# Last batch of a linear-attention layer: attention split by group of heads into the x buffers, output products in quarters, norms of unit 7 first

## The chip, the cores and the metric

One core of one Trainium2 chip runs the whole program. The metric is the device time of one execution in microseconds (us), lower is better. Engines: PE is TensorE (matmuls), DVE is VectorE, ACT is ScalarE, POOL is GpSimd, SP is SyncE (here it only issues DMAs).

## The reference, cut to what matters

Eight batches of 1024 tokens with 512 features, 16 heads of 32, 128 random features per head:

```python
q = feature_map(split(x @ Wq.T + bq), orf)      # exp(proj - norm) + EPS, norm from the row's squares
k = feature_map(split(x @ Wk.T + bk), orf)
v = split(x @ Wv.T + bv)
kv = jnp.einsum('nlm,nld->nmd', k, v)
ksum = jnp.sum(k, axis=1)
buf = jnp.concatenate([kv, ksum[..., None]], axis=-1)
out = jnp.einsum('nlm,nmd->nld', q, buf)
out = out[..., :-1] / out[..., -1:]
...
x = _layernorm(x + (out @ Wo.T + bo))
x = _layernorm(x + x @ (w_ternary * scale).T)
```

## The kernel before

**Units and groups.** The 16 heads are four groups of 4. Each group has two units of work: unit 2g makes the keys' features, unit 2g+1 the queries' features, so a batch has units 0 to 7. After unit 7 come the output stages, which take the 8 tiles of 128 tokens in turn.

**Order.** All engines walk one list, `SCHEDULE`, which `unit_stages` and `output_stages` write out; each engine does its own part of every stage, in that order, and waits on semaphores. The list decides what stands in front of what on each engine.

**Stages.** `P` projects a half unit into a bank of PSUM, in two parts of 6 matmuls. `S` (ACT) copies it as `unit_hi` and makes `squares`; `L` (DVE) makes `unit_lo`; `Q` (DVE) sums the squares; `N` (DVE) makes `norm_rows` from both sums. `LIFT` (SP's queue) moves hi and lo into `stacks`; `NL` (POOL's queue, 8 small DMAs) moves the norms there. A unit's feature stages `F` on PE wait for both. ACT takes the exponential of each `F` into `features`. For a key unit DVE adds the 8 tiles of features up (7 additions, L707 once and L710 six times, each waits for the one before). `G` are PE's products of features and values; the last of them (L910, "ones") also needs the sum of all 7 additions. ACT and PE then turn the result (`KVT`). `GG` is a half of a group's attention on PE, after which DVE turns and inverts the denominators (L783, L786, L789); `R` (L799, L801) writes a group's attention for four tiles (or, with a fourth number, two tiles) into `values_then_attention`.

**Output stages.** For each tile, `A` splits the attention into hi (ACT, L543) and lo (DVE, L715), and POOL adds the bias to the rows of x (L521); `O` is 12 matmuls with Wo; `LN` (DVE, L813 and L691 to L697) adds the rows and takes the statistics, POOL finishes the scale (L486, L488), ACT applies it (`Y`, L548); `YT` turns the tile (PE), ACT copies hi, DVE makes lo (L818); `FF` is 8 matmuls with the ternary weights, and DVE adds and takes statistics again (L823 and on); `ST` (ACT) scales and stores.

The hi and lo of `A` live in two slots each of `stacks`, so a tile's split waits for the output product two tiles back:

```python
if t < 2:
    act.wait_ge(t_f.sem, t_f.nth(b, 8 * NU))
else:
    act.wait_ge(t_o.sem, t_o.nth(b, t - 1))
```

In all but the last batch, unit 5 also splits the next batch's x (`XT`, on POOL for tiles 4 to 7, L515); the last batch has no such stages, and no projections of a next batch either.

Of the kernel before, what the change touches and what calls it, by code (L numbers as in the profile page):

```python
# [62 lines left out]
def unit_stages(b, u):  # L63
# [40 lines left out]
    if u < NU - 1:  # L104
# [3 lines left out]
        if u < NU - 3:  # L108
# [7 lines left out]
        return seq + [("R", b, g, 1)]  # L116
    v0 = [("V", b + 1, 0)] if two else []
# [4 lines left out]

def output_stages(b):

    more = b + 1 < B

    def v(t):
        return [("V", b + 1, t)] if more else []
# [3 lines left out]
    for t in range(3, TT):  # L132
# [4 lines left out]
        if t == 4 and more:  # L137
            seq += [("Q", b + 1, 1, 1), ("N", b + 1, 1)]
    seq += [("Y", b, TT - 1)] + v(TT - 1) + [("FF", b, TT - 2), ("ST", b, TT - 3), ("YT", b, TT - 1)]
    if more:  # L140
        return seq + [("P", b + 1, 2, 0, 0), ("P", b + 1, 2, 0, 1), ("LIFT", b + 1, 1), ("FF", b, TT - 1), ("NL", b + 1, 1)]
    return seq + [("FF", b, TT - 1), ("ST", b, TT - 2), ("ST", b, TT - 1)]
# [22 lines left out]
RING = {"V": "pj", "P": "pj", "O": "pj", "FF": "pj", "F": "ft", "YT": "ft"}  # L165
RING_SIZE = {"pj": 2, "ft": 3}


def bank_uses(seq):
# [3 lines left out]
    last = {ring: [(-1, None)] * size for ring, size in RING_SIZE.items()}  # L173
    held, out = {}, []
    for n, stage in enumerate(seq):
        ring = RING.get(stage[0])
        if stage[0] in ("S", "L"):
            out.append((held[("P", *stage[1:], 0)], None))
        elif stage[0] == "LN":
            out.append((held[("O", *stage[1:])], None))  # L180
        elif stage[0] == "P" and stage[4]:
            out.append((held[(*stage[:4], 0)], None))
        elif ring is None:
            out.append((None, None))
        else:
            mine = last[ring]
            bank = mine.index(min(mine, key=lambda use: use[0]))
            held[stage] = bank
            out.append((bank, mine[bank][1]))
            reader = {"P": ("L", *stage[1:4]), "O": ("LN", *stage[1:])}.get(stage[0], stage)  # L190
            mine[bank] = (at[reader], stage)
# [3 lines left out]
def attention_kernel(nc, x, xt, wq, wk, wv, wo, wff, bias, bo, orf, out):  # L195
# [5 lines left out]
    with ctx:  # L201
# [47 lines left out]
        BANKS = {"pj": PS[0:2], "ft": PS[2:5]}  # L249
# [35 lines left out]
        g_xb = Signal("x_plus_bias_ready", TT)  # L285
        g_ln = [Signal("ln1_scale_ready", 2 * TT), Signal("ln2_scale_ready", 2 * TT)]
# [46 lines left out]

        def x_rows(t):
# [3 lines left out]
        def old_bank(stage):  # L338
# [6 lines left out]
            if kind == "O":  # L345
                return v_ln[0], v_ln[0].nth(b, 5 * k + 1)
# [8 lines left out]
        def steps():  # L355

            for stage, (bank, old) in zip(SCHEDULE, BANKING):
                ps = None if bank is None else BANKS[RING.get(stage[0], "pj")][bank]
# [97 lines left out]
        def _(pool):  # L456
# [51 lines left out]
            for kind, b, at, _, _ in steps():  # L508
# [3 lines left out]
                elif kind == "XT" and b and t >= 4:  # L512
# [3 lines left out]
                                            ALU.subtract).then_inc(g_xlo.sem, 1)  # L516
                elif kind == "A":
# [10 lines left out]
        def _(act):  # L528
# [16 lines left out]
            def apply_norm(k, b, t):  # L545
                act.wait_ge(g_ln[k].sem, g_ln[k].nth(b, 2 * t + 2))
                row = XR[:, t % 4, :]
# [3 lines left out]
            for kind, b, at, ps, _ in steps():  # L551
# [61 lines left out]
                elif kind == "A":  # L613
                    split_hi(b, u)
                elif kind == "Y":
# [379 lines left out]
```

## Time and profile before

| | |
|---|---|
| median of 3 runs | 1331.96 us (1330.17 to 1334.98) |
| profiled execution | 1332.59 us, of which span 1330.8 us |
| PE busy | 96% of the span |
| DVE, ACT, POOL busy | 75%, 52%, 36% |
| last batch's units 5 to 7 and output stages | from about 1239 us to the end |

Times in the trace count from the start of the span. A busy PE is not PE at its peak, since matmuls overlap. `[idle before <-releaser]` at the end of a row is the engine's idle time ahead of it, and what ended it. The column PEclk is the granted TensorE clock, where 1.00 is 2.4 GHz and 0.50 is 1.2 GHz.

### The profile page before, as it was taken

The numbers are of one execution on the slowest core, as the hardware profiler recorded it, in microseconds if no ns is written. First come the engines' busy times: TensorE is split into PE (matmuls) and PEld (weight loads), VectorE is DVE, ScalarE is ACT, GpSimd is POOL, SyncE is SP. The second block draws the span as 40 slices with busy tenths as digits, with TensorE's granted clock in tenths as the row PEclk, the third lists the DMA queues.
The fourth block names the chain that finished last, engine by engine and source line by source line (L and its number), as shares of the span: only waits on it lengthen the run. The fifth ranks groups of instructions, "written<-read, shape, count | busy, mean of one in ns | idle before, by whom it ended". The sixth has DMA issues, their size and how long they took to land.

```text
span 1330.8 us, 25104 instructions
## 1 busy us (share of the span) xinstructions
PE 1280.9 (96%) x8522; PEld 962.9 (72%) x8522; DVE 996.5 (75%) x2077; ACT 695.6 (52%) x1337; POOL 476.1 (36%) x877
## 2 busy tenths in 40 slices
PE   6999999999999999999999999999999999999786
PEld 5766688677877768776787768876688667886564
DVE  5688875787767886688757887578876788758876
ACT  5466535565355643556436663366544664355543
POOL 1233432354333343234423343234442344332433
PEclk9999999999999999999999999999999999999999
DMA  5467503673146631468215662257602674046511
GB/s 205 128 144 195 137 33 96 170 190 93 52 110 167 174 87 54 107 159 209 60 56 127 170 170 67 60 138 203 156 25 75 168 192 122 33 116 138 139 47 48
DMA packets 94014, 160.35 MB, mean 120 GB/s; under 512 B 31168, under 2 KB 47680, under 8 KB 93376
## 3 DMA queue, kind: packets, MB, share of 16 engines
q1 hardware_dynamic: 67712, 139.51, 40.8%
q10 hardware_dynamic: 9792, 17.12, 3.4%
q0 software_dynamic: 16384, 2.13, 1.1%
q8 instruction: 68, 1.11, 0.4%
q14 instruction: 58, 0.48, 0.1%
HBM read 39.13 MB, written 16.78 MB: 42 GB/s over the span
## 4 chain that ended last, share of the span: by engine, by line
PE 81%; DVE 8%; ACT 4%; issue 3%; DMA 2%; SPq 2%; POOL 1%; ACTq 0%; DVEq 0%; POOLq 0%
PE ps L835 28%; PE ps L872 23%; PE ps L933 7%; PE ps L904 4%; PE ps L858 4%; PE ps L860 4%; PE ps L859 4%; PE ps L891 3%; PE ps L949 2%; ACT features L599 1%; DVE cols L786 1%; DVE squares_turned L753 1%; DVE cols L757 1%; DVE stacks L715 1%; ACT x_hi L568 1%
## 5 line engine op out<-in xcount | busy, mean ns | idle before, releaser
L599 ACT ACTIVATE features<-ps 128x512 f32<-128x512 f32 x512 | 278.6, 600 | 270.6 <-PE ps L835 198.6
L505 POOL DMA_DIRECT2D stacks<-norm_rows x512 | 252.0, 500 | 420.5 <-DVE norm_rows L768 169.4
L486 POOL TENSOR_TENSOR stats<-stats,cols 128x1 f32<-128x1 f32 x128 | 79.0, 617 | 377.9 <-DVE stats L697 377.9
L835 PE MATMUL ps<-Wo_hi,stacks 128*128 128x512 f32 x512 | 173.3, 402 | 5.8 <-DVE stacks L715 3.7
L710 DVE TENSOR_TENSOR den<-den,features 128x512 f32<-128x512 f32 x192 | 134.6, 701 | 15.4 <-ACT features L599 2.1
L573 ACT ACTIVATE values_then_attention<-ps 128x512 f32<-128x512 f32 x64 | 38.2, 598 | 200.2 <-PE ps L860 197.4
L835 PE MATMUL ps<-W_ternary,stacks 128*128 128x512 f32 x512 | 127.9, 392 | 6.9 <-DVE stacks L818 6.9
L835 PE MATMUL ps<-orf_key_a,stacks 128*128 128x256 f32 x512 | 132.3, 289 | 1.6 <-DMA stacks<-norm_rows 1.6
L933 PE MATMUL ps<-features,kv_ksum 128*32 128x512 f32 x1024 | 123.1, 598 | 8.4 <-ACT features L599 5.6
L835 PE MATMUL ps<-orf_key_b,stacks 68*128 68x256 f32 x512 | 129.0, 283 | 0.0
L548 ACT ACTIVATE rows<-rows,stats 128x512 f32<-128x512 f32 x128 | 100.9, 813 | 42.4 <-POOL stats L488 42.2
L835 PEld LDWEIGHTS ps<-Wo_hi,stacks 128*128 128x128 f32 x512 | 96.1, 188 | 35.5 <-DVE unit_lo L745 8.5
L835 PEld LDWEIGHTS ps<-orf_key_a,stacks 128*128 128x128 f32 x512 | 97.6, 191 | 27.5 <-issue 23.4
L835 PEld LDWEIGHTS ps<-W_ternary,stacks 128*128 128x128 f32 x512 | 96.0, 189 | 28.3 <-issue 4.7
L745 DVE SCALAR_TENSOR_TENSOR unit_lo<-ps,cols,unit_hi 128x512 fp32r<-128x512 f32 x128 | 94.2, 736 | 28.3 <-ACT squares L583 27.6
L858 PE MATMUL ps<-Wv_hi,x_hi 128*128 128x512 f32 x256 | 103.8, 406 | 11.7 <-DVE x_lo L738 10.9
L872 PE MATMUL ps<-x_hi,Wk_hi 128*128 128x512 f32 x256 | 106.9, 418 | 0.0
L872 PE MATMUL ps<-x_hi,Wq_hi 128*128 128x512 f32 x256 | 101.5, 396 | 2.1 <-DVE unit_lo L745 2.1
L872 PE MATMUL ps<-x_lo,Wq_hi 128*128 128x512 f32 x256 | 101.9, 398 | 0.0
L872 PE MATMUL ps<-x_hi,Wq_lo 128*128 128x512 f32 x256 | 101.4, 396 | 0.0
L872 PE MATMUL ps<-x_hi,Wk_lo 128*128 128x512 f32 x256 | 101.2, 395 | 0.0
L859 PE MATMUL ps<-Wv_lo,x_hi 128*128 128x512 f32 x256 | 101.0, 395 | 0.0
(113 smaller groups left out, 2615.6 us busy)
## 6 DMA issues: line engine op xcount, KB each, us to landing
stacks<-unit_hi SPq DMA_DIRECT2D x384, 128.0 KB, 2.5
stacks<-unit_lo SPq DMA_DIRECT2D x256, 128.0 KB, 3.3
stacks<-unit_hi SPq DMA_DIRECT2D x64, 256.0 KB, 3.8
out<-rows ACTq DMA_DIRECT2D x64, 256.0 KB, 2.0
rows<-in_x_t SPq DMA_DIRECT2D x56, 256.0 KB, 3.6
stacks<-norm_rows POOLq DMA_DIRECT2D x512, 4.0 KB, 2.6
rows<-in_x SPq DMA_DIRECT2D x32, 256.0 KB, 3.8
features<-in_x SPq DMA_DIRECT2D x32, 256.0 KB, 3.8
```

What stands on the lines that cost most here:

```text
L486: nc.gpsimd.tensor_tensor(ln(k, t, 10), ln(k, t, 8), EXPO, ALU.pow).then_inc(g_ln[k].sem, 1)
L505: pool.dma_start(slot[row:row + 1, c:c + L].rearrange("o (t c) -> o t c", c=DH), NN[DH * h:DH * (h + 1), u % 2, part, :].bitcast(F32)).the ...
L548: nc.scalar.activation(row, row, ACT.Identity, scale=ln(k, t, 10), bias=ln(k, t, 11))\
L599: nc.scalar.activation(FE[:, n % 8, :, 0:M], ps[:, :].rearrange("p (a m) -> p a m", a=HG), ACT.Exp, scale=C_EXP).then_inc(a_exp.sem, 1)
L710: ins = nc.vector.tensor_tensor(total, total, FE[:, r, :, 0:M], ALU.add)
L745: nc.vector.scalar_tensor_tensor(out=EL[:, u % 2, half], in0=ps[:, :], scalar=BC[:, u:u + 1], in1=EH[:, u % 2, half].bitcast(F32), op0=ALU ...
L835: last = mm(out, a, b, start=(n == 0), stop=(n == len(terms) - 1))
L858: mm(ps[:, :], XH[:, k, c], WH["v"][:, k, :], start=(k == 0), stop=False)
L859: mm(ps[:, :], XH[:, k, c], WL["v"][:, k, :], start=False, stop=False)
L860: last = mm(ps[:, :], XL[:, k, c], WH["v"][:, k, :], start=False, stop=(k == KT - 1))
L872: last = mm(ps[:, :], *terms[n], start=(n == 0), stop=(n == len(terms) - 1))
L933: last = mm(bank[DH * h:DH * (h + 1), :], KVS[:, g % 2, c + DH * h:c + DH * (h + 1)], FE[:, HG * half + h, :, 0:M], start=True, stop=True, ...
```

## The change

Only the last batch changes. In its unit 5, unit 7's projections, squares and norms come ahead of group 2's attention (`GG`, `R`). The attention of each group is split as soon as it exists (new stage `AG`), for four tiles at once, into the buffers `x_hi` and `x_lo`, which no projection needs any more: hi on ACT; lo on POOL for groups 0 to 2, and on DVE, two tiles at a time, for group 3. The output product of a tile is cut into four quarters (new stage `OK`, 3 matmuls for one group) that can run apart; the first ones run inside unit 7. The normed rows stay in `values_then_attention`, the turned ones go into `x_hi` and `x_lo`, and all five banks serve all of these stages. The order of the output stages is another one (`last_output_stages`).

```diff
-        if u < NU - 3:
+        if b + 1 == B and u == NU - 3:
+            seq += p[1] + s0 + l0 + kv + f(2, 3) + p[2] + f(4, 5) + s1 + q0 + [("KVT", b, g)] + f(6, 7) + l1 + [("GG", b, g, 0)] + q1 + norm + lift
+            seq += [("GG", b, g, 1), ("R", b, g, 0)] + [("LR", b, t) for t in range(4)]
+            seq += [("AG", b, k, h) for k in range(2) for h in range(2)]
+        elif u < NU - 3:
...
+    if b + 1 == B:
+        seq = [("AG", b, 2, 0), ("AG", b, 2, 1)] + f(0, 1, 2) + [("OK", b, 0, 0)] + kv + f(3) + [("OK", b, 1, 0), ("KVT", b, g)]
+        seq += f(4, 5) + [("A", b, t) for t in range(4)] + [("GG", b, g, 0), ("R", b, g, 0, 0), ("AG", b, g, 0, 0)] + f(6, 7)
+        seq += [("OK", b, t, k) for k in (1, 2) for t in (0, 1)] + [("R", b, g, 0, 1), ("AG", b, g, 0, 1)]
+        seq += [("OK", b, 0, 3), ("LN", b, 0), ("OK", b, 1, 3), ("LN", b, 1), ("GG", b, g, 1)]
+        seq += [("OK", b, 2, k) for k in range(KT)] + [("LN", b, 2), ("Y", b, 0), ("A", b, 4)]
+        return seq + [("LR", b, t) for t in range(4, TT)]
...
+def last_output_stages(b):
+
+    def o(t, *chunks):
+        return [("OK", b, t, k) for k in chunks or range(KT)]
+
+    g = NG - 1
+    seq = o(3) + [("R", b, g, 1, 0), ("AG", b, g, 1, 0), ("YT", b, 0), ("LN", b, 3), ("Y", b, 1), ("A", b, 5)]
+    seq += o(4, 0, 1, 2) + [("YT", b, 1), ("FF", b, 0), ("R", b, g, 1, 1), ("AG", b, g, 1, 1), ("Y", b, 2), ("A", b, 6), ("A", b, 7)]
+    for t in range(4, TT):
+        seq += o(t, 3) + [("LN", b, t)] + (o(t + 1, 0, 1, 2) if t + 1 < TT else []) + [("YT", b, t - 2), ("ST", b, t - 4), ("Y", b, t - 1), ("FF", b, t - 3)]
+    seq += [("YT", b, TT - 2), ("ST", b, TT - 4), ("Y", b, TT - 1), ("FF", b, TT - 3), ("YT", b, TT - 1), ("FF", b, TT - 2)]
+    return seq + [("ST", b, TT - 3), ("FF", b, TT - 1), ("ST", b, TT - 2), ("ST", b, TT - 1)]
...
+                elif kind == "AG" and t < NG - 1:
+                    tiles, c = group_tokens(t, at[1:])
+                    pool.wait_ge(a_ghi.sem, a_ghi.nth(0, 2 * t + at[1] + 1))
+                    nc.gpsimd.tensor_tensor(last_lo[:, tiles, c], VA[:, tiles, c], last_hi[:, tiles, c].bitcast(F32),
+                                            ALU.subtract).then_inc(g_glo.sem, 1)
...
+                elif kind == "AG":
+                    tiles, c = group_tokens(u, at[1:])
+                    if len(at) == 2:
+                        act.wait_ge(v_a.sem, v_a.nth(b, 2 * u + at[1] + 1))
+                        act.wait_ge(t_p.sem, t_p.nth(b, 2 * NU))
+                    else:
+                        act.wait_ge(v_a.sem, v_a.nth(b, 2 * u + at[1]) + at[2] + 1)
+                    nc.scalar.activation(last_hi[:, tiles, c], VA[:, tiles, c], ACT.Copy).then_inc(a_ghi.sem, 1)
...
+                elif kind == "AG" and u == NG - 1:
+                    tiles, c = group_tokens(u, at[1:])
+                    dve.wait_ge(a_ghi.sem, a_ghi.nth(0, 2 * u + 2 * at[1] + at[2] + 1))
+                    nc.vector.tensor_tensor(last_lo[:, tiles, c], VA[:, tiles, c], last_hi[:, tiles, c].bitcast(F32),
+                                            ALU.subtract).then_inc(v_glo.sem, 1)
...
+                elif kind == "OK":
+                    k = at[1]
+                    if k < NG - 1:
+                        pe.wait_ge(g_glo.sem, g_glo.nth(0, 2 * k + u // 4 + 1))
+                    else:
+                        pe.wait_ge(v_glo.sem, v_glo.nth(0, u // 2 + 1))
+                    a_hi, a_lo = (X[:, u, P * k:P * (k + 1)] for X in (last_hi, last_lo))
+                    mm(ps[:, :], a_hi, WH["o"][:, k, :], start=(k == 0), stop=False)
+                    mm(ps[:, :], a_hi, WL["o"][:, k, :], start=False, stop=False)
+                    last = mm(ps[:, :], a_lo, WH["o"][:, k, :], start=False, stop=(k == KT - 1))
+                    if k == KT - 1:
+                        last.then_inc(t_o.sem, 1)
```

**POOL, last batch, from unit 7's norms on.** Before, the norms' DMAs are followed by two bias additions of rows (tiles 0 and 1), and then by the first layer norm's scale:

```order
313 L505 DMA stacks<-norm_rows 1x32x32 x56
314 L521 TENSOR_TENSOR rows<-rows,out_bias 128x512 x2
315 L486 TENSOR_TENSOR stats<-stats,cols 128x1
316 L488 TENSOR_TENSOR stats<-stats 128x1
317 L521 TENSOR_TENSOR rows<-rows,out_bias 128x512
```

Now (L555 are the norms' DMAs, L570 the new lo of groups 0 to 2, L576 the bias additions):

```order
313 L555 DMA stacks<-norm_rows 1x32x32 x56
314 L570 TENSOR_TENSOR x_lo<-values_then_attention,x_hi 128x4x128 x6
315 L576 TENSOR_TENSOR rows<-rows,out_bias 128x512 x4
316 L536 TENSOR_TENSOR stats<-stats,cols 128x1
317 L538 TENSOR_TENSOR stats<-stats 128x1
```

Ten full-size operations with two inputs in SBUF stand in a row where there were two.

**DVE, last batch, unit 5.** Before, from unit 7's first lo (L745) to the first addition of unit 6's features; L768 ends the norms:

```order
1793 L799 STREAM_TRANSPOSE den<-cols 128x512
1794 L801 SCALAR_TENSOR_TENSOR values_then_attention<-ps,cols,den 128x4x128
1795 L753 STREAM_TRANSPOSE squares_turned<-squares 128x512
1796 L757 TENSOR_REDUCE cols<-squares_turned 128x16
1797 L745 SCALAR_TENSOR_TENSOR unit_lo<-ps,cols,unit_hi 128x512
...
1805 L768 TENSOR_TENSOR norm_rows<-norms_turned,norm_rows 128x32
1806 L799 STREAM_TRANSPOSE den<-cols 128x512
1807 L801 SCALAR_TENSOR_TENSOR values_then_attention<-ps,cols,den 128x4x128
1808 L707 TENSOR_TENSOR den<-features 128x512
1809 L710 TENSOR_TENSOR den<-den,features 128x512 x6
```

Now, from the end of the norms (L831) on:

```order
1800 L831 TENSOR_TENSOR norm_rows<-norms_turned,norm_rows 128x32
1801 L846 STREAM_TRANSPOSE den<-ps 128x512
1802 L849 TENSOR_SCALAR cols<-den,cols 128x16
1803 L852 RECIPROCAL cols<-cols 128x16
1804 L862 STREAM_TRANSPOSE den<-cols 128x512
1805 L864 SCALAR_TENSOR_TENSOR values_then_attention<-ps,cols,den 128x4x128
1806 L862 STREAM_TRANSPOSE den<-cols 128x512
1807 L864 SCALAR_TENSOR_TENSOR values_then_attention<-ps,cols,den 128x4x128
1808 L770 TENSOR_TENSOR den<-features 128x512
1809 L773 TENSOR_TENSOR den<-den,features 128x512 x6
```

Seven operations (a denominator and both `R`) moved from ahead of the norms' end to between it and the additions.

## Rows read from the trace of the kernel before

**Rows 1.** Stretches: length, busy us by engine, PEclk, DMA share, GB/s
```profile
1255.94:1262.67 6.73, 0.15 (x2) 0.03 (x1) 6.21 (x7) 0.78 (x2) 6.39 (x10) 0.76 0.69 203
1262.67:1266.20 3.53, 3.53 (x43) 2.34 (x43) 1.62 (x3) 1.09 (x2) 0.00 (x0) 0.50 0.00 0
1268.43:1330.80 62.37, 47.75 (x226) 34.93 (x226) 44.10 (x110) 23.67 (x36) 20.73 (x38) 0.95 0.15 51
```

**Rows 2.** Timeline of PE, last batch, units 6 and 7: start, length
```profile
1255.80 0.28 PE L835 MATMUL ps<-orf_key_b,stacks 68*128 68x256 f32 x1
1262.67 1.19 PE L891 MATMUL ps<-stacks,orf_query 98*128 98x512 f32 x2 [6.59 <-DMA stacks<-norm_rows]
...
1265.52 0.65 PE L910 MATMUL ps<-den,ones 128*32 128x128 f32 x8
...
1268.43 1.93 PE L933 MATMUL ps<-features,kv_ksum 128*32 128x512 f32 x16
```

**Rows 3.** Timeline of POOL, the same stretch
```profile
1255.94 3.91 POOL L505 DMA_DIRECT2D stacks<-norm_rows  x8 [9.68 <-PE ps L835]
1259.87 2.48 POOL L521 TENSOR_TENSOR rows<-rows,out_bias 128x512 f32<-128x512 f32 x2
```

**Rows 4.** Timeline of ACT and DVE, last batch, units 5 and 6
```profile
1245.95 0.68 ACT L583 ACTIVATE squares<-ps,cols 128x512 f32<-128x512 f32 x1
...
1251.46 0.74 DVE L745 SCALAR_TENSOR_TENSOR unit_lo<-ps,cols,unit_hi 128x512 fp32r<-128x512 f32 x1
...
1255.17 0.19 DVE L768 TENSOR_TENSOR norm_rows<-norms_turned,norm_rows 128x32 fp32r<-128x32 f32 x1
...
1256.75 0.68 DVE L707 TENSOR_TENSOR den<-features 128x512 f32<-128x512 f32 x1
...
1259.93 2.98 DVE L710 TENSOR_TENSOR den<-den,features 128x512 f32<-128x512 f32 x1
```

**Rows 5.** Timeline of DVE, POOL and ACT in earlier batches
```profile
308.23 0.98 POOL L505 DMA_DIRECT2D stacks<-norm_rows  x2
308.74 0.23 DVE L786 TENSOR_SCALAR cols<-den,cols 128x16 f32<-128x16 f32 x1
...
471.07 3.42 DVE L786 TENSOR_SCALAR cols<-den,cols 128x16 f32<-128x16 f32 x1
471.91 2.53 POOL L521 TENSOR_TENSOR rows<-rows,out_bias 128x512 f32<-128x512 f32 x2
...
772.44 2.54 POOL L515 TENSOR_TENSOR x_lo<-rows,x_hi 128x512 fp32r<-128x512 f32 x2 [0.80 <-ACT x_hi L568]
772.64 1.12 DVE L786 TENSOR_SCALAR cols<-den,cols 128x16 f32<-128x16 f32 x1
772.93 0.63 ACT L568 ACTIVATE x_hi<-rows 128x512 fp32r<-128x512 f32 x1 [0.57 <-DMA rows<-in_x_t]
```

**Rows 6.** Timeline of SP's queue, the lift of unit 7, its last four
```profile
1253.75 2.42 SPq L453 DMA_DIRECT2D stacks<-unit_lo  x4
```

**Rows 7.** Timeline of DVE from the last group's attention to the end
```profile
1270.41 0.72 DVE L783 STREAM_TRANSPOSE den<-ps 128x512 f32<-128x512 f32 x1 [2.15 <-PE ps L933]
...
1271.72 0.45 DVE L799 STREAM_TRANSPOSE den<-cols 128x256 f32<-128x256 f32 x1
...
1290.28 0.69 DVE L813 TENSOR_TENSOR rows<-ps,rows 128x512 f32<-128x512 f32 x1
...
1292.20 0.74 DVE L823 SCALAR_TENSOR_TENSOR rows<-ps,cols,rows 128x512 f32<-128x512 f32 x1
...
1294.16 0.68 DVE L818 TENSOR_TENSOR stacks<-ps,stacks 128x512 fp32r<-128x512 f32 x1
1294.76 0.44 DVE L799 STREAM_TRANSPOSE den<-cols 128x256 f32<-128x256 f32 x1
...
1295.63 1.21 DVE L715 TENSOR_TENSOR stacks<-values_then_attention,stacks 128x512 fp32r<-128x512 f32 x1
...
1326.36 0.14 DVE L697 TENSOR_SCALAR stats<-stats 128x1 f32<-128x1 f32 x1
```

More of the change, by code:

```diff
@@ L120, in unit_stages @@
     return seq + [("LR", b, t) for t in range(4, TT)]
+def last_output_stages(b):
[8 more added lines that the diff above has]
+    return seq + [("ST", b, TT - 3), ("FF", b, TT - 1), ("ST", b, TT - 2), ("ST", b, TT - 1)]
 def output_stages(b):
     more = b + 1 < B
+    if not more:
+        return last_output_stages(b)
     def v(t):
-        return [("V", b + 1, t)] if more else []
+        return [("V", b + 1, t)]
     seq = [("O", b, 0), ("LN", b, 0), ("A", b, 2), ("R", b, NG - 1, 1, 0), ("O", b, 1), ("LN", b, 1), ("Y", b, 0), ("A", b, 3)]
@@ L162, with ring @@
     SCHEDULE += output_stages(_b)
-RING = {"V": "pj", "P": "pj", "O": "pj", "FF": "pj", "F": "ft", "YT": "ft"}
-RING_SIZE = {"pj": 2, "ft": 3}
+RING = {"V": (0, 1), "P": (0, 1), "O": (0, 1), "FF": (0, 1), "F": (2, 3, 4), "YT": (2, 3, 4)}
+def ring(stage):
+    if stage[0] == "OK":
+        return (0, 1) if stage[2] < 2 else (0, 1, 2, 3, 4)
+    if stage[0] in ("YT", "FF") and stage[1] + 1 == B:
+        return (0, 1, 2, 3, 4)
+    return RING.get(stage[0])
 def bank_uses(seq):
     at = {stage: n for n, stage in enumerate(seq)}
-    last = {ring: [(-1, None)] * size for ring, size in RING_SIZE.items()}
+    last = [(-1, None)] * 5
     held, out = {}, []
     for n, stage in enumerate(seq):
-        ring = RING.get(stage[0])
         if stage[0] in ("S", "L"):
@@ L179, in bank_uses @@
         elif stage[0] == "LN":
-            out.append((held[("O", *stage[1:])], None))
+            out.append((held.get(("O", *stage[1:]), held.get(("OK", *stage[1:], 0))), None))
         elif stage[0] == "P" and stage[4]:
             out.append((held[(*stage[:4], 0)], None))
-        elif ring is None:
+        elif stage[0] == "OK" and stage[3]:
+            out.append((held[(*stage[:3], 0)], None))
+        elif ring(stage) is None:
             out.append((None, None))
         else:
-            mine = last[ring]
-            bank = mine.index(min(mine, key=lambda use: use[0]))
+            bank = min(ring(stage), key=lambda k: last[k][0])
             held[stage] = bank
-            out.append((bank, mine[bank][1]))
-            reader = {"P": ("L", *stage[1:4]), "O": ("LN", *stage[1:])}.get(stage[0], stage)
-            mine[bank] = (at[reader], stage)
+            out.append((bank, last[bank][1]))
+            reader = {"P": ("L", *stage[1:4]), "O": ("LN", *stage[1:]), "OK": ("LN", *stage[1:3])}.get(stage[0], stage)
+            last[bank] = (at[reader], stage)
     return out
@@ L332, in x_stage, with normed, group_tokens, turned_rows @@
             return flat.rearrange("p (k c) -> p k c", k=KT)
+        def normed(b, t):
+            return XR[:, t % 4, :] if b + 1 < B else VA[:, t, :]
+        last_hi, last_lo = (X[:, :, :].rearrange("p k (s d) -> p (k s) d", d=D) for X in (XH, XL))
+        def group_tokens(g, at):
+            t0, n = (4 * at[0], 4) if len(at) == 1 else (4 * at[0] + 2 * at[1], 2)
+            return slice(t0, t0 + n), slice(P * g, P * (g + 1))
+        def turned_rows(b, t):
+            if b + 1 < B:
+                return ST[:, 1, 2048:2560], ST[:, 1, 2560:3072]
+            return last_hi[:, t, :], last_lo[:, t, :]
         def x_rows(t):
@@ L357, in steps @@
             for stage, (bank, old) in zip(SCHEDULE, BANKING):
-                ps = None if bank is None else BANKS[RING.get(stage[0], "pj")][bank]
+                ps = None if bank is None else PS[bank]
                 yield stage[0], stage[1], stage[2:], ps, old
```

43 lines of the change are left out of this document (22 added, 21 removed).

## The prediction, made before the changed kernel ran

> **What bounds the kernel now.** I read the table by stages first. Batches 0 to 6 keep their order, and PE is nearly always busy there; all that can move is the last batch from unit 5 on. There I read PE's timeline for its holes. The largest is between unit 6 and unit 7: PE's last key product starts at 1255.80, and its next matmul at 1262.67, after 6.59 us in which it waits for the norms' DMAs [rows 2]. The hole has an aftermath: over the next 3.5 us the granted clock is 0.50, which is 1.2 GHz [rows 1]. Then come 62.4 us from the first half of the last group's attention (1268.43) to the end of the span, in which PE is busy for 47.8 and DVE for 44.1 [rows 1]: neither is full, they hand tiles to each other, and the engines' order decides how much of the 62.4 is waiting.
>
> **Step 1, the norms come earlier.** Unit 7's second lo starts at 1251.46 on DVE, though ACT's squares, its last input, were there at 1245.95 + 0.68 = 1246.63 [rows 4]: what stands ahead on DVE is group 2's denominators and R. In the new order these come later. ACT has the squares a little later than before (it now takes them between other copies), so I put L745 at 1247.15, with 1246.65 as lower bound. That is 4.3 us earlier, and all that hangs on it moves too: the norms' last operation from 1255.17 [rows 4] to 1250.9, the eight norm DMAs, which take 3.93 us to POOL's next instruction at 1259.87 [rows 3], to 1251.65 to 1255.55, and unit 7's first matmul to 1262.67 - 4.3 = 1258.4. SP's lift of unit 7 ends its issues at 1253.75 + 2.42 = 1256.2 [rows 6]; it can't start before unit 7's hi, some 1.5 us earlier than now, so it ends at 1254.7 and has 3.7 us to land. I take the norms as the later of the two. By itself this step is worth 4.3 us, and perhaps some of the clock.
>
> **Step 2, what now stands behind the norms on POOL.** Ten TENSOR_TENSORs with both inputs in SBUF follow at 1255.55: six new lo and four bias additions. All that they wait for is there in time: groups 0 and 1 are old, group 2's hi comes by about 1258, and POOL asks for it only after four others. One takes 2.53 / 2 = 1.27 us [rows 5], ten take 12.7. On DVE, meanwhile, group 2's denominators (1271.72 - 1270.41 = 1.3 us [rows 7]) and two R (1.47 each: 1256.75 - 1255.17 is one of them and a gap [rows 4]) come between the norms and the additions, so the first addition starts at 1250.9 + 4.35 = 1255.25, 0.3 us ahead of POOL's chain. It ends at 1255.95.
>
> These two don't run side by side. An addition takes 0.8 us from start to start, (1259.93 - 1256.75) / 4 [rows 4]. The one at 1259.93 took 2.98 us, just where POOL ran two bias additions, to 1262.35 [rows 3, 4]. It ended 0.56 us behind both, and did not get in between them. The same is seen in the third batch: a TENSOR_SCALAR of 0.23 us took 3.42, through the rest of the DMAs' issue and both bias additions [rows 5]; it is one of four such meetings in the trace. It did get in once, at 772.64: there POOL's second operation waited for ACT's copy, which ended at 772.93 + 0.63 = 773.56, barely before the first operation did at 773.71 [rows 5]. So where POOL's next operation has been released in time, DVE waits for it too; where it hasn't, DVE gets in. Here all ten are released in time. I take the wait for the whole chain: additions 2 to 7 run from 1255.95 + 12.65 = 1268.6, the second ends at 1269.2, and five more at 0.8 end at 1273.15.
>
> The Trainium skill, SBUF — State Buffer, section "Who interferes with whom", says that a VectorE instruction with two SBUF inputs contends with a GpSimd instruction that reads SBUF, and that whoever is first holds the pair for its whole instruction. The trace agrees that they exclude each other; read to the letter, the rule frees the pair after each instruction, which would give the alternation that is the second rival below, 5.7 us less than my sum.
>
> **Step 3, to the last group's attention.** PE's "ones" products need the seventh addition. Before they started at 1265.52, and the attention at 1268.43, 2.9 us later [rows 2]. Unit 7's first three F, one quarter of an output product and four G run from 1258.4 to 1260.9, and then PE is idle for 12 us, longer than in the old hole, so I count the clock at 0.50 again. An F and a quarter product (3 matmuls) now stand between the ones and the turn: 0.6 us more at the low clock. The attention starts at 1273.2 + 2.9 + 0.6 = 1276.7, which is 8.3 us later than before.
>
> **Step 4, from there to the end.** DVE is the fuller engine. It starts 1270.41 - 1268.43 = 2.0 us behind PE [rows 2, 7]. A layer norm's statistics take 1292.20 - 1290.28 = 1.92 us, the FF's 1.96, a y_lo 0.60 and half an R 0.87 [rows 7]. Eight of each of the first three are 35.8, four half R 3.5, two denominators 2.6. The eight lo of 0.68 go, for four of half the size on DVE, not seen before: with the 0.44 of another operation of this size [rows 7] as lower and 0.68 as upper bound, 0.5, together 2.0. Sum 44. Waits that I find by walking the new order with these lengths: 0.9 for ACT's hi of group 3's first half, 1.2 for the lo of tiles 4 and 5 beside the bias addition of tile 4, 2.5 for the lo of tiles 6 and 7 beside those of tiles 6 and 7, which now stand together on POOL (one such meeting before: 1.21 in place of 0.68 at 1295.63 [rows 7]), and 2.3 at the end, where ACT stores tile 4 ahead of Y of tile 7: together 6.9. After the last statistics the span has 1330.8 - 1326.5 = 4.3 us left [rows 1, 7], unchanged. 2.0 + 44 + 6.9 + 4.3 = 57.2, against 62.4: 5.2 us less. The quarter products cost PE nothing in themselves: as many matmuls as before, two quarters of them ahead of this stretch. PE's 47.8 less those is below DVE's chain.
>
> **Sum.** +8.3 - 5.2 = +3.1 us on a span of 1330.8. The profiled execution took 1332.59, 1.8 more than its span and 0.6 above the median; I put the difference on the median: 1331.96 + 3.1 = 1335.1. What a measurement of this kernel can tell from no change is 0.3%, or 4.0 us. My own range for this case is 1331 to 1340: step 4's walk knows no small latencies (up to 3 us more), L745 may be 0.5 earlier, and POOL may start first, which blocks the first addition as well (+0.8).
>
> **Rivals.**
> *The additions are not held up.* Were the 2.98 us something else, the seventh addition would end at 1255.25 + 6 x 0.8 + 0.7 = 1260.7, PE would have "ones" at 1260.9 and the attention at 1264.0 (with a little low clock): 4.4 us earlier than before, and -9.6 us in all: 1322.4. For it: in the last batch's second additions POOL's DMAs alone slow nothing (the additions from 1256.75 to 1259.93 ran beside them [rows 3, 4]). Against it: the row at 1259.93.
> *The engines alternate.* DVE gets in behind each POOL operation: six turns of 1.27 + 0.68 from 1255.95 end at 1267.65, the attention starts at 1271.0, 2.6 us later than before: -2.6, 1329.4. It decides whether POOL's successor holds what its predecessor had. For it: 772.64; against: 1259.93 and 471.07 [rows 4, 5].
> *Slower.* Group 2's second denominator (a TENSOR_SCALAR, 0.23 us) comes at 1251.7, just as POOL's norm DMAs begin. At 308.74 it ran beside such DMAs in 0.23 us, at 471.07 it was held through the last 0.8 us of them [rows 5]. If it is held from the first DMA on, it waits for the DMAs and four lo, to 1260.6; R and the additions follow it (group 2's hi is then late, and breaks POOL's chain once), POOL's other six end at 1271.5, the additions at 1276.0, and the attention starts at 1279.5: +6.0, 1338.0. What decides is whether that TENSOR_SCALAR is issued before POOL's first DMA or after it, and whether a DMA far from the end of its row holds it.
>
> **How the numbers follow.** The chain held: 0.50, 1335.1. Alternation: 0.22, 1329.4. Not held up: 0.20, 1322.4. Denominator held: 0.08, 1338.0. Faster (below 1328.0): all of the 0.20 and 0.04 of the alternation. Slower (above 1336.0): 0.08 and 0.22 of the first case, whose value lies only 1 us below that bound. No change: the other 0.46. The range of 8 in 10 runs from 1321, to take in the third case's value, to 1339.
>
> **What will show it.** Right: POOL has ten operations of 1.27 us without a gap behind the norms' DMAs; one addition of unit 6 on DVE takes 12 to 13 us; PE idles between G and "ones" in unit 7 and not at unit 7's first F, which starts some 4 us earlier; "ones" waits for the additions. From the last group's attention to the end there are 57 us, and the lo of tiles 6 and 7 takes 2 us or more. Wrong: six additions of 2 us each (alternation), or all of 0.7; a lift that lands after the norms; or a stretch to the end that is as long as before, if ACT's order delays Y.

## The result, and the profile after

| | before | changed |
|---|---|---|
| median of 11 runs each | 1331.96 us (1329.25 to 1334.98) | 1337.54 us (1332.44 to 1340.59) |
| ratio, with its 95% interval | | 1.0031 (1.0017 to 1.0046) |
| profiled execution's span | 1330.8 us | 1337.1 us |

The changed kernel is slower by 0.3%: 4.1 us by the ratio, 5.6 by the medians. The prediction had 1335.1 us, in a range from 1321 to 1339, and forecast +3.1.

Batches 0 to 6 run the same code, yet the last batch starts at another moment in each profiled execution. So this text measures inside the last batch: from PE's first `F` of unit 5 to the last group's attention ("start"), and from there to the end of the span ("end"). The two first rows are from PE's timeline of the kernel before and of the changed one (start, length in us):

```profile
1239.32 0.63 PE L891 MATMUL ps<-stacks,orf_query 98*128 98x512 f32 x2
```

```profile
1241.40 0.63 PE L963 MATMUL ps<-stacks,orf_query 98*128 98x512 f32 x2
...
1259.73 0.94 PE L963 MATMUL ps<-stacks,orf_query 98*128 98x512 f32 x3 [1.27 <-DMA stacks<-norm_rows]
1261.75 1.95 PE L976 MATMUL ps<-features,values_then_attention 128*32 128x129 f32 x32
1275.62 0.65 PE L982 MATMUL ps<-den,ones 128*32 128x128 f32 x8 [11.93 <-DVE den L773]
...
1279.49 2.75 PE L1005 MATMUL ps<-features,kv_ksum 128*32 128x512 f32 x16
```

Before, start was 1268.43 - 1239.32 = 29.1 us and end 62.4 [rows 1, 2]. Now they are 1279.49 - 1241.40 = 38.1 and 57.6. Together 95.7 against 91.5: 4.2 us more, what the ratio says too. The hole of 6.59 us ahead of unit 7's first `F` [rows 2] has shrunk to 1.27, and a new one of 11.93 us stands ahead of the ones products. PE waits there for DVE. POOL's and DVE's timelines of the changed kernel, the answers to [rows 3, 4], say why:

```profile
1254.03 3.91 POOL L555 DMA_DIRECT2D stacks<-norm_rows  x8 [5.68 <-PE ps L907]
1257.96 7.40 POOL L570 TENSOR_TENSOR x_lo<-values_then_attention,x_hi 128x512 fp32r<-128x512 f32 x6
1265.33 4.91 POOL L576 TENSOR_TENSOR rows<-rows,out_bias 128x512 f32<-128x512 f32 x4
```

```profile
1249.38 0.75 DVE L808 SCALAR_TENSOR_TENSOR unit_lo<-ps,cols,unit_hi 128x512 fp32r<-128x512 f32 x1 [1.40 <-ACT squares L638]
...
1253.25 0.19 DVE L831 TENSOR_TENSOR norm_rows<-norms_turned,norm_rows 128x32 fp32r<-128x32 f32 x1
...
1257.45 13.34 DVE L770 TENSOR_TENSOR den<-features 128x512 f32<-128x512 f32 x1
1270.89 4.67 DVE L773 TENSOR_TENSOR den<-den,features 128x512 f32<-128x512 f32 x6
```

One addition, 0.68 us by itself [rows 4], lasts 13.34 us: it is issued 0.5 us before POOL's norm DMAs end, and it ends 0.55 us behind the last of POOL's ten operations (1265.33 + 4.91 = 1270.24). The six others run freely behind it. The stages of the changed kernel, as in [rows 1]:

```profile
1255.00:1268.00 13.00, 7.24 (x87) 5.28 (x85) 12.79 (x5) 3.81 (x8) 12.98 (x16) 0.85 0.52 142
1268.00:1280.00 12.00, 4.38 (x20) 2.55 (x24) 7.53 (x9) 3.88 (x11) 2.23 (x2) 0.50 0.00 0
1280.00:1337.10 57.10, 46.56 (x220) 33.54 (x212) 41.33 (x106) 20.05 (x31) 16.67 (x36) 0.95 0.16 56
```

DVE counts as busy for 12.79 of the first 13 us, but from 1257.45 on it only waits inside one instruction. In the second stretch, with the end of the hole in it, the clock is granted at 0.50, 1.2 GHz; in the attention's first half (1279.49 to 1282.24) it is 0.69 on average, and that half takes 2.75 us where it took 1.93 [rows 2]. DVE's timeline of the output stages, against [rows 7]:

```profile
1282.32 0.72 DVE L846 STREAM_TRANSPOSE den<-ps 128x512 f32<-128x512 f32 x1 [3.15 <-PE ps L1005]
...
1295.84 0.97 DVE L874 TENSOR_TENSOR x_lo<-values_then_attention,x_hi 128x256 fp32r<-128x256 f32 x1 [0.48 <-ACT x_hi L677]
...
1303.22 0.95 DVE L874 TENSOR_TENSOR x_lo<-values_then_attention,x_hi 128x256 fp32r<-128x256 f32 x1 [0.48 <-ACT x_hi L677]
...
1325.85 0.75 DVE L895 SCALAR_TENSOR_TENSOR values_then_attention<-ps,cols,values_then_attention 128x512 f32<-128x512 f32 x1 [1.99 <-PE ps L907]
...
1332.68 0.14 DVE L760 TENSOR_SCALAR stats<-stats 128x1 f32<-128x1 f32 x1
```

### The profile page after: what moved, and what is told of

Its sections match the earlier page's. It is cut to its first block, busy times and chain, and to the rows that moved or that the text cites. A ratio compares the mean times of both kernels' runs of the same rounds, so it can differ in the third digit from the quotient of the medians.

```text
span 1337.1 us, 25110 instructions
## 1 busy us (share of the span) xinstructions
PE 1280.4 (96%) x8522; PEld 961.8 (72%) x8522; DVE 1008.8 (75%) x2073; ACT 695.9 (52%) x1339; POOL 481.8 (36%) x883
## 4 chain that ended last, share of the span: by engine, by line
PE 78%; DVE 10%; ACT 3%; issue 3%; SPq 3%; DMA 2%; POOL 0%; ACTq 0%; DVEq 0%; POOLq 0%
PE ps L907 27%; PE ps L944 22%; PE ps L1005 7%; PE ps L930 4%; PE ps L976 4%; PE ps L932 4%; PE ps L931 4%; PE ps L963 3%; PE ps L1033 2%; DVE cols L849 1%; DMA rows<-in_x_t 1%; ACT features L654 1%; DVE den L770 1%; SPq L503 1%; SPq L492 1%
## 5 line engine op out<-in xcount | busy, mean ns | idle before, releaser
L555 POOL DMA_DIRECT2D stacks<-norm_rows x512 | 251.9, 500 | 414.1 <-DVE norm_rows L831 180.8
L907 PE MATMUL ps<-Wo_hi,stacks 128*128 128x512 f32 x448 | 151.6, 402 | 7.9 <-DVE stacks L778 7.2
L907 PE MATMUL ps<-W_ternary,stacks 128*128 128x512 f32 x448 | 110.7, 389 | 0.0
L907 PEld LDWEIGHTS ps<-Wo_hi,stacks 128*128 128x128 f32 x448 | 84.1, 188 | 33.8 <-DVE unit_lo L808 12.8
L603 ACT ACTIVATE rows<-rows,stats 128x512 f32<-128x512 f32 x112 | 87.9, 812 | 26.0 <-POOL stats L538 26.0
L944 PE MATMUL ps<-x_lo,Wk_hi 128*128 128x512 f32 x256 | 100.7, 394 | 0.0
L932 PE MATMUL ps<-Wv_hi,x_lo 128*128 128x512 f32 x256 | 100.7, 393 | 0.0
```

The lines of the kernel that those rows point to most:

```text
L555: pool.dma_start(slot[row:row + 1, c:c + L].rearrange("o (t c) -> o t c", c=DH), NN[DH * h:DH * (h + 1), u % 2, part, :].bitcast(F32)).the ...
L603: nc.scalar.activation(row, row, ACT.Identity, scale=ln(k, t, 10), bias=ln(k, t, 11))\
L907: last = mm(out, a, b, start=(n == 0), stop=(n == len(terms) - 1))
L932: last = mm(ps[:, :], XL[:, k, c], WH["v"][:, k, :], start=False, stop=(k == KT - 1))
L944: last = mm(ps[:, :], *terms[n], start=(n == 0), stop=(n == len(terms) - 1))
```

## The experiments

The theory: DVE's additions are held by POOL's whole row of two-input operations. Rivals: the engines take turns and something else delays the start; or the norms' new place or the new output order costs the time. Twelve kernels; times in us, ratios with 95% intervals, each against executions of the kernel before that were timed along with it (their medians are 1331.96 to 1333.91). Start and end come from one profiled execution of each kernel. Where the interval includes 1 (e2, e4, e6), the times show no change, and only the trace tells the kernels apart:

| kernel | median | ratio | start | end | sum |
|---|---|---|---|---|---|
| before | | 1 | 29.1 | 62.4 | 91.5 |
| changed | 1337.54 | 1.0031 (1.0017 to 1.0046) | 38.1 | 57.6 | 95.7 |
| e1 gate | 1326.52 | 0.9945 (0.9923 to 0.9967) | 29.5 | 57.2 | 86.7 |
| e2 rows early | 1333.41 | 0.9993 (0.9974 to 1.0011) | 33.1 | 57.5 | 90.6 |
| e3 memsets | 1323.0 | 0.9924 (0.9884 to 0.9965) | 26.0 | 56.7 | 82.7 |
| e4 norms only | 1333.07 | 0.999 (0.9971 to 1.0009) | 26.7 | 64.6 | 91.2 |
| e5 memset and wait | 1327.83 | 0.9967 (0.9944 to 0.999) | 30.8 | 57.7 | 88.6 |
| e6 own waits | 1329.75 | 0.9988 (0.997 to 1.0005) | 32.4 | 57.5 | 89.9 |
| e7 lo on DVE | 1328.1 | 0.9955 (0.9937 to 0.9972) | 25.1 | 61.4 | 86.5 |
| e8 all but the norms | 1336.49 | 1.003 (1.0012 to 1.0048) | 39.7 | 57.8 | 97.5 |
| e9 gate, rows early | 1328.47 | 0.9965 (0.9951 to 0.9979) | 29.8 | 56.7 | 86.5 |
| e10 and late stores | 1326.41 | 0.9953 (0.9937 to 0.9969) | 29.4 | 54.9 | 84.3 |
| e11 memset, no wait | 1337.79 | 1.0031 (1.0013 to 1.0049) | 38.1 | 56.8 | 94.9 |
| e12 all edits | 1323.76 | 0.9928 (0.9911 to 0.9944) | 24.5 | 57.2 | 81.7 |

**e1, the gate.** POOL's six lo wait for the seventh addition:

```diff
                     pool.wait_ge(a_ghi.sem, a_ghi.nth(0, 2 * t + at[1] + 1))
+                    pool.wait_ge(v_ks.sem, v_ks.nth(b, 7 * NG))
```

> The changed kernel with one wait more: POOL starts each of its six new lo only after unit 6's seventh addition. Times below are counted from PE's first F of unit 5 in the last batch to the end of the span (before 91.5 us, changed kernel 95.7). If a row of POOL operations holds the SBUF reads that DVE needs: the seven additions take 0.8 us each (5.5 us in all, in place of 18.1), and the hold moves on to the next DVE instruction that wants them, the TENSOR_SCALAR ahead of the turn of unit 6's products, which waits 8 to 10 us for POOL's ten operations; the last group's attention starts about 3.5 us earlier than in the changed kernel: 92.2 us. If the first addition's 13.3 us came from something else about it (a late input, DMA traffic), either it stays or the small operation is not held: 83 to 85 us, or 95.7.

DVE's timeline:

```profile
1257.77 0.68 DVE L771 TENSOR_TENSOR den<-features 128x512 f32<-128x512 f32 x1
1258.55 4.67 DVE L774 TENSOR_TENSOR den<-den,features 128x512 f32<-128x512 f32 x6
...
1269.88 0.96 DVE L840 TENSOR_SCALAR cols<-cols 128x2 f32<-128x2 f32 x1 [6.65 <-ACT kv_ksum_t L667]
```

The seven additions run freely, the first beside the last 0.5 us of the same DMAs (1254.35 to 1258.26), and in the trace the kernel gains 9.0 us on the changed one, 8.6 of them in its start. That settles that POOL's row is the cause. The sum is 86.7, where 92.2 was expected. The small TENSOR_SCALAR at 1269.88, in the middle of that row, took 0.96 us and not the 8 to 10 expected: it had only one of POOL's operations to wait for. So "released in time" does not suffice for a hold. What differs is that POOL had waited 5.13 us for the seventh addition, between its DMAs and the row.

**e2, rows early.** The bias additions of tiles 0 to 3 are issued in unit 3; only the six lo follow the norms' DMAs:

```diff
+        if u == 2 and b + 1 == B:
+            seq += [("LR", b, t) for t in range(4)]
...
+            seq += [("A", b, t) for t in range(4) if b + 1 == B and u == 3]
```

> The changed kernel, but the loads of the last batch's rows 0 to 3 are issued in unit 2 and their four bias additions run on POOL in unit 3, so that POOL's row behind the norms has six operations and not ten. If the hold lasts as long as the row: the first addition takes 6 x 1.23 + 1 = 8.4 us and not 13.3, everything behind it comes 4.9 us earlier, 90.8 us from unit 5's first F to the end, and the whole is 0.1% below the kernel before. If the hold ended after a fixed time or with the first POOL operations, the first addition would keep its 13.3 us or fall to about 2.

DVE's timeline:

```profile
1257.83 8.46 DVE L773 TENSOR_TENSOR den<-features 128x512 f32<-128x512 f32 x1
```

Four operations of 1.23 us fewer, and the hold is 4.9 us shorter: it is as long as the row, as expected.

**e3, memsets.** The six lo become memsets, which read nothing (the low halves of groups 0 to 2 are left out of the result):

```diff
-                    nc.gpsimd.tensor_tensor(last_lo[:, tiles, c], VA[:, tiles, c], last_hi[:, tiles, c].bitcast(F32),
-                                            ALU.subtract).then_inc(g_glo.sem, 1)
+                    nc.gpsimd.memset(last_lo[:, tiles, c].bitcast(F32), 0.0).then_inc(g_glo.sem, 1)
```

> The changed kernel, but POOL's six new lo for groups 0 to 2 are set to zero (a memset that reads nothing of SBUF) and not computed: the low halves of these groups are left out of the result. The four bias additions, which read, follow. If DVE's additions wait for POOL's reads: the first additions run in 0.7 us beside the memsets, and one of them takes some 5.5 us, through the four bias additions; the last group's attention starts 7 to 11 us earlier than in the changed kernel. If any POOL operation holds them off, the first addition waits through memsets and bias additions alike, 8 to 12 us. The time of a memset of this size has no row so far; I expect 0.4 to 1.2 us.

POOL's timeline, then one line's instructions on DVE (durations in ns, shortest, median and longest):

```profile
1252.68 2.88 POOL L570 MEMSET x_lo<- 128x512 f32 x6
1255.65 6.17 POOL L575 TENSOR_TENSOR rows<-rows,out_bias 128x512 f32<-128x512 f32 x4
```

```profile
L772 DVE TENSOR_TENSOR den<-den,features x6: 691/692/1581, 1253.0 to 1257.9; 128x512 f32<-128x512 f32 x6
```

The additions run freely beside the memsets, and the start is 26.0, more of a gain (12.0) than the 7 to 11 expected. The expected wait of 5.5 us through the four bias additions did not come: with them DVE takes turns (1.58 at most), although no wait for an operation of POOL's own stands there.

**e4, norms only.** The kernel before, with unit 5 alone in the new order (the first hunk of the change, without `AG`).

> The kernel before with only unit 5 of the last batch in the new order (no split by group, no quarters). Unit 7's first F starts 4.3 us earlier. Of that the path keeps what the additions leave: they start 1.5 us earlier than before, and two bias additions on POOL hold one of them for 2.5 us, so they end at 1263.3 in the frame of the kernel before, and PE's ones products start there and not at 1265.5: 2.1 us faster in all, 89.4 us from unit 5's first F to the end, ratio 0.9984. If the additions were not held: 4.3 us or a little more with the clock. If the new order costs something of its own: no gain.

PE's timeline:

```profile
1254.60 0.71 PE L894 MATMUL ps<-stacks,orf_query 98*128 98x512 f32 x2 [2.07 <-DMA stacks<-norm_rows]
...
1258.80 0.66 PE L913 MATMUL ps<-den,ones 128*32 128x128 f32 x8 [2.11 <-DVE den L713]
...
1262.12 3.64 PE L936 MATMUL ps<-features,kv_ksum 128*32 128x512 f32 x16
```

and its stretch from 1262 to 1266, as in [rows 1]:

```profile
1262.00:1266.00 4.00, 4.00 (x18) 0.91 (x18) 0.17 (x1) 0.89 (x2) 0.00 (x0) 0.50 0.01 4
```

Unit 7's first `F` comes 1254.60 - 1235.46 = 19.1 us after unit 5's, where it was 23.4: 4.2 earlier, the step-1 price. The start gains 2.4 of them, the end gives 2.2 back: 1.7 of it in this first half at the low clock (3.64 against 1.93). Expected was a sum of 89.4, it is 91.2: earlier norms alone are worth nothing that the times can tell.

POOL's row says something more. These are the two bias additions of the kernel before, but here POOL had to wait 2.92 us for the load of their rows behind the norms' DMAs, and they start at 1254.91 and take 3.28 us. Nothing is held through both of them, as the addition at 1259.93 was before [rows 4]: the two that DVE runs beside them take 1.58 and 1.57 us. So a wait of POOL for something else than its own operation gives turns too.

**e8, all but the norms.** The changed kernel with unit 5 in the old order.

> The changed kernel with unit 5 of the last batch in the order of before (norms late), split by group and quarters kept. POOL's ten operations then start 4.3 us later, when four of the seven additions are through; one of the later ones is held for some 12 us. The last group's attention starts 38 to 39 us after unit 5's first F, as in the changed kernel, and the whole is 95 to 97 us: the earlier norms gain nothing as long as POOL's row follows them. If the earlier norms did their part (4.3 us), this one would take 100 us.

One line's instructions on DVE:

```profile
L773 DVE TENSOR_TENSOR den<-den,features x6: 691/692/13562, 1262.1 to 1279.0; 128x512 f32<-128x512 f32 x6
```

Here three additions run freely beside the DMAs (1260.54 to 1264.45); the one issued at 1263.73, 0.7 us before these end, is held for 13.56. By the times, the change without the early norms costs as much (1.003), so with the row in place the norms give nothing that can be told. In the trace its sum is 1.8 us above the changed kernel's (95 to 97 was expected), but this is the second longest of its ten executions, 1343.2 against a median of 1336.49.

**e5 and e11, one memset, with and without a wait.** Behind unit 7's norm DMAs POOL writes one unused column. In e5 it then waits for that memset's own end:

```diff
                 if kind == "NL":
                     lift_norms(b, t)
+                    if b + 1 == B and t == NU - 1:
+                        nc.gpsimd.memset(col(60), 0.0).then_inc(s_own, 1)
+                        pool.wait_ge(s_own, 1)
```

> The changed kernel with one tiny POOL operation (a memset of one column) after the eight norm DMAs, whose end POOL waits for before its row of ten. The first run with a wait (POOL after the additions) showed that a small DVE operation got in after one POOL operation of a row of ten, so a row as such does not hold. What is left: the row holds when it is queued straight behind the DMAs. If that is so, the first addition now waits for one POOL operation at most (2 us or less), additions and POOL take turns, the seventh ends some 4 to 7 us earlier than in the changed kernel: 89 to 92 us from unit 5's first F to the end. If a row of operations that are all released in time holds by itself (the theory of the prediction), the first addition keeps its 13 us.

In e11 the memset stays, and `then_inc` and the wait go:

> The changed kernel with a memset of one column behind unit 7's norm DMAs on GpSimd, as in the kernel in which GpSimd also waited for that memset's end (there the engines took turns), but without the wait. If it is the wait that brings the turns back (the row is held because it follows the DMAs without GpSimd's parts coming together), the first held addition takes 12 us or more again, and the time is that of the changed kernel: 94 to 96 us from unit 5's first F to the end. If any instruction of another kind between DMAs and row is enough, the additions take turns at 1.7 us each: 88 to 90.

POOL and DVE in e5, then in e11:

```profile
1254.35 0.12 POOL L564 MEMSET cols<- 128x1 f32 x1
1254.56 9.65 POOL L574 TENSOR_TENSOR x_lo<-values_then_attention,x_hi 128x512 fp32r<-128x512 f32 x6
...
1253.87 0.68 DVE L774 TENSOR_TENSOR den<-features 128x512 f32<-128x512 f32 x1
1254.65 10.11 DVE L777 TENSOR_TENSOR den<-den,features 128x512 f32<-128x512 f32 x6
```

```profile
1257.60 0.12 POOL L563 MEMSET cols<- 128x1 f32 x1
1257.66 7.41 POOL L572 TENSOR_TENSOR x_lo<-values_then_attention,x_hi 128x512 fp32r<-128x512 f32 x6
...
1257.13 13.37 DVE L772 TENSOR_TENSOR den<-features 128x512 f32<-128x512 f32 x1
```

Without the wait, the same ten operations of POOL hold one addition for 13.37 us. With it, the first addition is through before the row begins, and the six others take turns with the row (1.69 us an addition, 1.61 an operation of POOL). The wait costs 0.15 us on POOL (0.21 against 0.06 from the memset to the row) and gives 6.3 us back (94.9 to 88.6). The memset alone changes nothing: 1.0031, as the changed kernel. The times agree with the traces (0.9967 against 1.0031, in intervals that don't meet).

**e6, own waits.** Each of POOL's ten operations waits for the end of its own predecessor:

```diff
                     pool.wait_ge(a_ghi.sem, a_ghi.nth(0, 2 * t + at[1] + 1))
+                    pool.wait_ge(g_glo.sem, g_glo.nth(0, 2 * t + at[1]))
```

> The changed kernel, in which each of POOL's ten operations but the first waits for the end of the one before it (nothing stands between the DMAs and the first). If a row queued behind the DMAs holds because POOL goes from one operation to the next without a gap, the first addition is let in behind the first POOL operation (2 us), and additions and POOL take turns: 89 to 92 us from unit 5's first F to the end. If it is the DMAs ahead of the row that make the hold, whatever stands between the operations, it stays at 13 us.

Turns again (the first addition 2.36 us, the others 1.66 each). Its sum is 1.3 us more than that of e5, so one wait at the row's head does at least as much as a wait between all of them.

**e7, lo on DVE.** Rows early, the lo of groups 0 to 2 on DVE in two parts behind each half of the attention (`AL`), and the first quarter products behind the attention: POOL has nothing there.

> The changed kernel with nothing on POOL behind the norms' DMAs: rows 0 to 3 and their bias additions early (as in the run with rows early), and the lo of groups 0 to 2 on DVE, those of tiles 0 to 3 after the turn of unit 6's products and those of tiles 4 to 7 after the second denominator; all quarters of the output products after the first half of the last group's attention. The additions then end 5.5 us after their start; the last group's attention starts 24.3 us after unit 5's first F (before 29.1, changed kernel 38.1), the way to the end is 60 us (changed kernel 57.6; 2.1 for the late lo, the rest for the quarters): 84.5 us in all, ratio 0.995. If DVE's six new lo (0.7 each) were on the path in full, 87 us.

The start is the shortest so far, 25.1, but the end is 61.4. Six lo of 0.63 us are new on DVE, the fuller engine, the moved products are new on PE, and the attention's first half took 3.12 us at a clock of 0.61 on average; no run tells these three apart.

**e9, gate and early rows**, the edits of e1 and e2.

> The changed kernel with both earlier edits: GpSimd's six lo wait for the seventh addition, and the bias additions of tiles 0 to 3 are issued two units earlier. With only the gate the last group's attention began 29.5 us after unit 5's first F, with only the rows early 33.1, and with no work for GpSimd there 25.1. Theory of the hold: the start of the additions is free as with the gate, unit 7's small TENSOR_SCALAR is before GpSimd's row, and the second denominators meet six operations (7.4 us) and not ten, so the attention begins at 26.5 to 29.5 and the stretch behind it stays 57.2 to 57.6: 84 to 87 us from unit 5's first F to the end, 0.990 to 0.995 of the time before. Rival: the lo of groups 0 and 1, now behind the additions, come too late for the output products, and the stretch behind the attention grows by what the start gains: 88 or more, no better than the gate alone (86.7).

The start stays at 29.8. PE's timeline names the next wait:

```profile
1261.57 0.77 PE L1029 MATMUL ps<-Wo_hi,x_hi 128*128 128x512 f32 x1 [3.40 <-POOL x_lo L574]
```

The quarter product of tile 0 stands ahead of `G` and the ones products, and now waits for POOL's gated lo. In e1 it waited 2.25 us too. The early rows add nothing to the gate that can be told: 0.9965 against 0.9945.

**e10, late stores.** As e9, with `Y` ahead of `ST` in the last stages:

```diff
-        ... [("YT", b, t - 2), ("ST", b, t - 4), ("Y", b, t - 1), ("FF", b, t - 3)]
+        ... [("YT", b, t - 2), ("Y", b, t - 1), ("ST", b, t - 4), ("FF", b, t - 3)]
```

> The same, and in the last stages ACT normalizes the next tile (Y) before it stores the tile of the FF ahead of it (ST). The prediction counted 2.3 us of waiting at the end for the store of tile 4 ahead of Y of tile 7: if so, the stretch from the last group's attention to the end is 1 to 2.3 us shorter than in the kernel with the same start and the old order. Rival: the late stores and their FF (which waits for the store's read of a row) give it back, no difference within 0.5 us.

The end is 1.8 us shorter in the profile, and the wait of 1.69 us that DVE has in e9 for PE's `FF` of tile 5 is gone. By the times alone (0.9953 against 0.9965) the difference is not told apart from nothing.

**e12, all edits.** As e10, with the first two quarter products behind the attention:

```diff
-        seq = ... + f(0, 1, 2) + [("OK", b, 0, 0)] + kv + f(3) + [("OK", b, 1, 0), ("KVT", b, g)]
+        seq = ... + f(0, 1, 2) + kv + f(3) + [("KVT", b, g)]
-        seq += [("OK", b, t, k) for k in (1, 2) for t in (0, 1)] + ...
+        seq += [("OK", b, t, k) for k in (0, 1, 2) for t in (0, 1)] + ...
```

> The kernel with the gate, the early rows and the later stores, and the two quarter products of group 0 now stand behind the last group's attention instead of ahead of the ones products. In the kernel before this edit PE waited 4.25 us for GpSimd's lo of group 0 there, and the attention began 29.4 us after unit 5's first F and 54.9 us before the end. If that wait sets the start, the attention begins at 25 to 26, as where GpSimd had no row at all, and the end is 55 to 56.5 us later (two quarter products more in it): 80.5 to 82.5 us, ratio 0.990 to 0.993. Rival: the DVE, busier in that stretch, already set the end, or the attention meets GpSimd's six operations: then 83 to 84.5, and no more than 1 us of gain.

PE's timeline:

```profile
1242.42 0.63 PE L967 MATMUL ps<-stacks,orf_query 98*128 98x512 f32 x2
...
1263.94 0.42 PE L986 MATMUL ps<-den,ones 128*32 128x128 f32 x8 [1.89 <-DVE den L777]
...
1266.94 3.12 PE L1009 MATMUL ps<-features,kv_ksum 128*32 128x512 f32 x16 [0.20 <-DVE kv_ksum L838]
```

The start is 24.5, and this kernel, at 0.9928, is 0.7% faster than the kernel before and 1.0% faster than the changed one (0.9928 / 1.0031). The end is longer than the 55 to 56.5 expected; 1.2 us of it is the attention's first half, 3.12 us at the low clock where e10 took 1.92. The edits carry what the change was able to give: the attention starts 4.6 us earlier than before, and the end is 5.2 shorter.

## Why the prediction was right, step by step

**Step 1 held.** The second lo is at 1249.38, which is 2.08 less in the time of before (the shift of unit 5's first `F`): 1247.30, predicted 1247.15. Unit 7's first `F` is at 1257.65 in that time, predicted 1258.4. What did not hold is the 4.3 us that the step was said to be worth by itself: alone it brought 0.2 us in the trace and nothing in the times (e4), because the additions then set the start, and the low clock took from the end.

**Step 2 held in its size, but its reason was wrong in part, and that was luck.** The ten operations take 12.3 us (predicted 12.7), and one addition waits for all of them. It was the first and not the second. The range has that case, with +0.8, but only if POOL starts first; POOL did not: the addition was issued 0.51 us ahead of POOL's row and was held all the same.

The prediction took from the rows of before that DVE waits whenever POOL's next operation has been released in time [rows 5]. e1 and e5 show otherwise: there the whole row was released too, and DVE got in behind one operation. The held cases that it read all had their row straight behind POOL's DMAs, and so had the changed kernel; that is why a rule that is too broad gave the right size.

What the runs single out is whether POOL waits between its DMAs and the row. Without a wait, the row holds DVE to its end (the changed kernel, e2, e8, e11). With one, they take turns, whether POOL waits for its own operation (e5, in 0.15 us), for DVE (e1, and e12, where a TENSOR_SCALAR of 1.03 us got in behind the second of six) or for a load (e4). Waits between the operations do it too (e6). e5 and e11 are the clean pair, since they differ in nothing but the wait.

Why a wait does this is not shown. The Trainium skill, GPSIMD Engine Reference, section "Instruction dispatch", says that the parts of GpSimd don't wait for each other between instructions, and that each begins the next one when its own share is done, while a semaphore waits for all. A reading that fits: after the DMAs the parts run apart, somebody always holds the port, and a wait brings them together. The runs agree with it (13.37 against 1.69 us), but no trace shows the parts.

The rule of the Trainium skill, SBUF — State Buffer, section "Who interferes with whom", that whoever is first gets the pair for its whole instruction, fits e5 and e6 if it is read as freeing the pair after each instruction; the changed kernel, e2, e8 and e11 contradict that reading. That it excepts a GpSimd instruction that only writes agrees with e3.

**Step 3 held.** Start grew by 9.0 us, predicted 8.3. Since the first addition was held, six and not five follow the row: the ones products began at 1273.54 in the time of before, 0.3 later than predicted, and the turned result, with the clock at 0.50, took 1279.49 - 1275.62 = 3.9 us from the ones products to the attention, predicted 3.5.

**Step 4 held as a sum, its terms less.** 57.6 us against 57.2. The lo of tiles 6 and 7 took 0.95 us, 0.5 over its own 0.44 and not 2.5 over it, the prediction's term: it had to wait for one of the two bias additions alone. Those of tiles 4 and 5 took 0.97 (0.5 of waiting where 1.2 was predicted). Against this the denominators came 2.83 us behind the attention instead of 2.0, at a clock of 0.69, and DVE waited some 0.4 us at a time for PE's `FF`, which the walk didn't hold (0.40 and 0.47 ahead of tiles 2 and 3). At the end DVE waited 1.99 us for PE, predicted 2.3; e10 agrees with its cause, the store ahead of `Y`, by 1.8 us in the trace.

**The sum** was 4.2 in the trace, predicted 3.1: 0.7 too little in the start, 0.4 in the end. The largest single miss is that of lo beside the bias additions (2.7 us too much in step 4), which DVE's late start, its waits for PE and small latencies made up for. That these cancel, and leave 0.4 us in the end, is luck.

**The rivals.** No hold at all, priced with a start 4.4 us shorter than before, is what e12 comes near to (4.6 shorter, with two quarter products moved out of it). Alternation, priced at 1329.4, is e5 in all but the wait: start 30.8 - 29.1 = 1.7 later than before (priced 2.6), sum 2.9 less (priced 2.6). The denominator was not held: its TENSOR_SCALAR was issued at 1254.11, 0.08 us after the first DMA, and took 0.23 us.

## What to carry to other kernels

Before two-input operations are moved to GpSimd, look at what stands ahead of them on its queue and what VectorE does meanwhile: right behind GpSimd-issued DMAs a row of them can cost VectorE the length of the whole row, and a wait of GpSimd for an operation of its own at the row's head turns that into one operation at a time. Or gate the row behind VectorE's urgent work (86.7 against 88.6 us here, by the trace), and then look at who was waiting for the row. A gain in one stretch (here 5.2 us) shows only when the loss in the other is undone, so measure both from a common moment inside the trace.

## What was not expected

- Whether VectorE's operation is held depends on when it is issued: at 0.5 to 0.7 us before the DMAs' end it is held, at 1.5 us before it runs in 0.69 us (e8). With no row directly behind, 0.5 us before is harmless (e1). The small TENSOR_SCALAR of batches 0 to 6, which meets a row of two behind such DMAs, draws the line closer: in the kernel before it is held for 3.4 us when issued 0.83 us before the DMAs' end (at 148.29, 471.07 and 950.70), and takes 0.23 us at 0.88 and 0.95 before (631.49 and 308.74). Issued 0.41 us into the row, at 1111.97, it still waits 2.18 us, to the end of both operations.
- In e3 the engines took turns without any wait in the code behind the memsets. The last two memsets ask for hi that ended at 1254.3 and 1254.9, about when they were due, so POOL may have waited there for an instant; no row shows it, and it stays open.
- TensorE's clock in the attention's first half. In e4, behind waits of 2.07 and 2.11 us, ahead of 1254.60 and 1258.80, it is granted at 0.50, and in e12 at 0.60, as its row of 1266.9 to 1270 shows:

```profile
1266.90:1270.00 3.10, 3.06 (x17) 0.60 (x17) 0.00 (x0) 0.55 (x2) 3.10 (x3) 0.60 0.02 5
```

  That half took 3.64 and 3.12 us, against 1.93 before. Yet in e1, e9 and e10, where PE waited 2.25, 3.40 and 4.25 us at one place shortly ahead of it, and in e11, behind a hole of 12.97 us, the clock there is 1.00 and the half takes 1.92. The changed kernel and e11 differ by 0.83 us in this half and by 0.8 in the sum. The clock can take back part of a gain at this place; when it does is not settled by these runs.
